# Moving the table entries of the last items of a routed attention block, and two of its ranks, to other places in GpSimd's, TensorE's and VectorE's order

## The reference

```python
gates = softmax(flat @ Wgate)                 # flat: 4096 tokens (in items of 256), 8 experts
_, top_inds = top_k(gates, 2)
mask = zeros((N, E), bool).at[arange(N)[:, None], top_inds].set(True)
pos = cumsum(mask, axis=0) * mask - 1         # the rank of a token in its expert
exp_in = zeros((E, capacity, d)).at[e_flat, p_eff].set(flat[t_flat])
exp_out = gelu(exp_in @ W1 + b1) @ W2 + b2
moe = zeros((N, d)).at[t_flat].add(exp_out[e_flat, p_g] * gate)
```

## Time and profile before

| | us |
|---|---|
| median of 3 runs | 1511.07 (1511.07 to 1511.7) |
| the profiled execution's own time | 1514.36 |
| its span, first to last instruction | 1512.6 |
| TensorE busy | 1397.3 (92%) |
| VectorE busy | 1063.2 (70%) |
| ScalarE busy | 898.2 (59%) |
| GpSimd busy | 651.4 (43%) |

### The profile page before, as it was taken

One profiled execution on the slowest core, in us unless ns is written; L12 is line 12 of the kernel. 1 busy time (PEld: TensorE's weight loads), 2 busy tenths in 40 slices (PEclk: granted clock), 3 DMA queues, 4 the chain that ended last, 5 costly groups with the idle time before them and its releaser, 6 DMA issues.

```text
span 1512.6 us, 26340 instructions
## 1 busy us (share of the span) xinstructions
PE 1397.3 (92%) x9265; PEld 1190.9 (79%) x9265; DVE 1063.2 (70%) x2514; ACT 898.2 (59%) x2092; POOL 651.4 (43%) x624
## 2 busy tenths in 40 slices
PE   7987899999999999999999998998729999999997
PEld 5765789999999998777876776776518888888886
DVE  2998577777777776778897787885436666666654
ACT  5776355555555553378887887887626455465452
POOL 0222344344343414555556665553434435445333
PEclk9998899999999999999999999999759999999999
DMA  6421256666665633343453454442432443234212
GB/s 176 140 81 37 60 155 170 171 177 178 172 186 170 171 102 124 100 142 116 133 147 100 135 142 102 123 123 71 126 85 58 93 102 95 38 98 100 40 22 29
DMA packets 133587, 173.53 MB, mean 115 GB/s; under 512 B 20725, under 2 KB 105536, under 8 KB 133456
## 3 DMA queue, kind: packets, MB, share of 16 engines
q1 hardware_dynamic: 105296, 119.89, 24.4%
q0 software_dynamic: 28160, 51.96, 17.3%
HBM read 107.28 MB, written 42.08 MB: 99 GB/s over the span
## 4 chain that ended last, share of the span: by engine, by line
PE 74%; DVE 8%; issue 6%; DMA 5%; ACT 3%; POOL 2%; another core or an unknown queue 1%; SPq 1%; POOLq 0%; DVEq 0%; ACTq 0%
PE banks L941 33%; PE banks L1983 8%; PE banks L1470 5%; PE banks L1514 4%; DMA xe<-pooled,idx 4%; PE banks L1985 4%; PE banks L1567 4%; PE banks L1003 3%; PE banks L451 2%; PE banks L1527 2%; PE banks L1488 1%; PE banks L1529 1%; PE banks L1959 1%; DVE row_at L516 1%
## 5 line engine op out<-in xcount | busy, mean ns | idle before, releaser
L941 PE MATMUL banks<-hi_x,hi_w 128*128 128x320 f32 (+1 forms) x832 | 289.4, 348 | 9.9 <-DVE hidden L976 5.3
L941 PE MATMUL banks<-lo_x,hi_w 128*128 128x320 f32 (+1 forms) x832 | 287.6, 346 | 0.0
L941 PE MATMUL banks<-hi_x,lo_w 128*128 128x320 f32 (+1 forms) x832 | 287.6, 346 | 0.0
L882 POOL DMA_INDIRECT xe<-pooled,idx x160 | 159.1, 995 | 235.1 <-DVE hidden L976 104.4
L1618 ACT ACTIVATE PN<-banks,smax 128x256 f32<-128x256 f32 (+1 forms) x512 | 180.3, 443 | 11.9 <-DVE smax L1724 11.9
L1443 POOL DMA_INDIRECT got<-done,slot x128 | 125.6, 981 | 143.3 <-DVE smax L1724 71.4
L1983 PE MATMUL banks<-down_w,hi_h 128*128 128x512 f32 x512 | 183.8, 401 | 0.0
L1944 POOL DMA_INDIRECT out<-X,tab x64 | 100.1, 1565 | 187.1 <-DVE X L2048 157.7
L941 PEld LDWEIGHTS banks<-hi_x,hi_w 128*128 128x128 f32 x832 | 159.6, 192 | 25.1 <-issue 8.0
L941 PEld LDWEIGHTS banks<-hi_x,lo_w 128*128 128x128 f32 x832 | 159.3, 192 | 13.7
L941 PEld LDWEIGHTS banks<-lo_x,hi_w 128*128 128x128 f32 x832 | 159.7, 192 | 12.3
(11 more groups left out here) (194 smaller groups left out, 3299.7 us busy)
## 6 DMA issues: line engine op xcount, KB each, us to landing
w<-in_L_ffn_w SPq DMA_DIRECT2D x96, 256.0 KB
done<-res SPq DMA_DIRECT2D x31, 640.0 KB
BIG<-in_L_ffn_W SPq DMA_DIRECT2D x16, 1024.0 KB
QS<-parts_qk SPq DMA_DIRECT2D x48, 256.0 KB
KS<-parts_qk SPq DMA_DIRECT2D x96, 128.0 KB
mask<-in_c_masks SPq DMA_DIRECT2D x16, 257.0 KB, 2.9
pooled<-XF SPq DMA_DIRECT2D x16, 256.0 KB, 3.2
WS<-in_L_cond_W SPq DMA_DIRECT2D x16, 256.0 KB
```

The source lines that it names most:

```text
L882: e.indirect_dma_start(xe[:, n % NXE, i, :], None, pooled, bass.IndirectOffsetOnAxis(ap=idx0[:, n * NS0 + i:n * NS0 + i + 1], axis=0)).the ...
L941: last = e.matmul(o, a[i], b[j], start=start and k == 0, stop=stop and k == 2, skip_group_check=True)
```

## The change

The tables change, and the step "entry" gets two more names, so that one table can hold an item's entries at two places.

- POOL_ROUND gets ("late", -3, 1 to 3) and ("ahead", -2, 0 and 1) between ("base", -2) and the gathers. The dictionary spread names those entries of items 10 to 13 that run there in place of their old places: (10, 1 to 3), (11, 1 to 3), (12, 1 to 3), (13, 0) and (13, 1). Each of them, and (13, 2) and (13, 3) in the drain, also waits for a given count of row maxima (one, (12, 2), for a count of gate logits).
- Of the eight (14, i), those with i = 1, 3, 5 and 7 wait for the outputs of item 15 turned (s_o_ps 31), scaled (s_at 32), turned back (s_at_turned 16) and for its projection (s_proj 16).
- In the drain the four (15, i) stand ahead of ("norm", 15, 1) instead of behind it.
- ("rank", 14) moves ahead of ("values", 15, 2) and ("gate", 14), ("rank", 15) ahead of ("proj", 15); ("place", 14) moves ahead of the last row maximum, ("place", 15) ahead of VectorE's ("proj", 15).

```diff
 POOL_ROUND
-        ("got", 3, 0, 3), ("got", 3, 1, 0), ("norm", -1, 1), ("got", 3, 1, 1), ("norm", 2, 0), ("entry", -3, 1),
+        ("late", -3, 1), ("late", -3, 2), ("late", -3, 3), ("ahead", -2, 0), ("ahead", -2, 1), ("got", 3, 0, 3), ("got", 3, 1, 0), ("norm", -1, 1), ("got", 3, 1, 1), ("norm", 2, 0), ("entry", -3, 1),
 POOL_LAST
-        *(("entry", 13, i) for i in range(TB * K1)), *(("entry", 14, i) for i in range(R * K1)), ("norm", 15, 1),
-        *(("entry", 15, i) for i in range(TB * K1)), *(("entry", 16, i) for i in range(TB * K1)))
+        ("entry", 13, 2), ("entry", 13, 3), *(("entry", 14, i) for i in range(R * K1)), *(("entry", 15, i) for i in range(TB * K1)),
+        ("norm", 15, 1), *(("entry", 16, i) for i in range(TB * K1)))
@@
+    ENTRY_PACE14 = {1: (s_o_ps, TB * 15 + 1), 3: (s_at, TB * 15 + 2), 5: (s_at_turned, 16), 7: (s_proj, 16)}
+    LATE = B - 6
+    entry_pace = {(b, i): (s_smax, 3 * NG * (b + 3) + n) for b in range(LATE, B - 4) for i, n in ((1, 1), (2, 4), (3, 6))}
+    entry_pace.update({
+        (12, 1): (s_smax, 3 * NG * 15), (12, 2): (s_lgs, 14), (12, 3): (s_smax, 3 * NG * 15 + 1), (13, 0): (s_smax, 3 * NG * 15 + 4),
+        (13, 1): (s_smax, 3 * NG * 15 + 7), (13, 2): (s_smax, 3 * NG * 15 + 10), (13, 3): (s_smax, 3 * NG * 15 + 12)})
+
+    spread = {a: "late" for a in entry_pace if a[0] < 13}
+    spread.update({(13, 0): "ahead", (13, 1): "ahead"})
@@
-            elif step == "entry" and entry_at(b, d[0]):
+            elif step in ("entry", "late", "ahead") and step == spread.get((b, d[0]), "entry") and entry_at(b, d[0]):
...
+                if (b, d[0]) in entry_pace:
+                    e.wait_ge(*entry_pace[b, d[0]])
+                if b == 14 and d[0] in ENTRY_PACE14:
+                    e.wait_ge(*ENTRY_PACE14[d[0]])
```

More of the change, by code:

```diff
@@ L1211, in _build @@
         ("scores", 15, 3, 0), ("turn_p", 15, 2, 2), ("scores", 15, 3, 1), ("values", 15, 1), ("turn_p", 15, 2, 0),
-        ("turn_p", 15, 2, 1), ("gate_turn", 14), ("scores", 15, 3, 2), ("values", 15, 2), ("gate", 14),
-        ("turn_p", 15, 3, 2), ("rank", 14), ("turn_p", 15, 3, 0), ("turn_p", 15, 3, 1), ("values", 15, 3),
-        ("outputs", 15, 0), ("outputs", 15, 1), ("out_turn", 15), ("proj", 15), ("rank", 15), ("gate_turn", 15),
-        ("gate", 15), ("rank", 16))
+        ("turn_p", 15, 2, 1), ("gate_turn", 14), ("scores", 15, 3, 2), ("rank", 14), ("values", 15, 2), ("gate", 14),
+        ("turn_p", 15, 3, 2), ("turn_p", 15, 3, 0), ("turn_p", 15, 3, 1), ("values", 15, 3),
+        ("outputs", 15, 0), ("outputs", 15, 1), ("out_turn", 15), ("rank", 15), ("proj", 15),
+        ("gate_turn", 15), ("gate", 15), ("rank", 16))
     DVE_LAST = (
         ("route", 13, 3), ("row_max", 15, 2, 0), ("proj", 14), ("row_max", 15, 2, 1), ("norm", 14, 1),
-        ("row_max", 15, 2, 2), ("scale", 14, 1), ("row_max", 15, 3, 0), ("row_max", 15, 3, 1), ("row_max", 15, 3, 2),
-        ("base", 14), ("gate", 14), ("route_shift", 14), ("place", 14), ("route", 14, 1), ("outputs", 15, 0), ("outputs", 15, 1),
-        ("route", 14, 2), ("route", 14, 3), ("proj", 15), ("norm", 15, 1), ("base", 15), ("scale", 15, 1), ("place", 15), ("gate", 15),
-        ("route_shift", 15), ("route", 15, 1), ("route", 15, 2), ("route", 15, 3), ("place", 16))
+        ("row_max", 15, 2, 2), ("scale", 14, 1), ("row_max", 15, 3, 0), ("row_max", 15, 3, 1), ("place", 14),
+        ("row_max", 15, 3, 2), ("base", 14), ("gate", 14), ("route_shift", 14),
+        ("route", 14, 1), ("outputs", 15, 0), ("outputs", 15, 1), ("route", 14, 2), ("route", 14, 3), ("place", 15),
+        ("proj", 15), ("norm", 15, 1), ("base", 15), ("scale", 15, 1), ("gate", 15), ("route_shift", 15), ("route", 15, 1),
+        ("route", 15, 2), ("route", 15, 3), ("place", 16))
     ACT_LAST = (
```

## The result

The changed kernel takes 1502.98 us as the median of 10 runs (1501.45 to 1508.52) and the kernel before 1511.46 beside it (10 runs, 1507.16 to 1515.7). The ratio is 0.995, 95% interval 0.9936 to 0.9964, so 5.4 to 9.7 us are gained, where 3.4 were forecast. The profiled execution took 1504.43 us, 9.9 less than the one of before.

The account below looks back on a forecast made before the run. TensorE was taken to bound the full rounds, a chain of waits the drain. T at -8.0 us (-1.0, -3.5, -3.5) and the norm at +4.6 gave -3.4: 1507.7 us as median, chance 0.45, range 1503.5 to 1514.0.

Parts of the forecast that it names:

- the stall at 1023.49 gone: Round 13: moving (10, 1 to 3) from behind the norms removes oT's 1.10 us wait; 1.0 us gained.
- round 15: Rounds 14 and 15: breaking up the run of four entries from 1046.62 gains 3.5 us, bounds 0 and 5.9.
- drain up to T: Drain before item 15's outputs: fewer entries there shorten waits of a row maximum and a weights copy; 3.5 us gained.
- T: Moment VectorE can start on item 15's outputs, 1090.14 before; forecast 8.0 us sooner, between 1080 and 1084.
- place 14 ahead of the last row maximum: Drain, VectorE: seven small instructions of 1.13 us, hidden by ScalarE's exponentials; cost 0, at most 1.2 us.
- norm of item 15: Drain, GpSimd: eleven entries ahead of it make it start at T + 14.0, not T + 9.4; 4.6 us lost.
- a bound of 6.0 us: Most the drain up to T could gain: 17.40 us less TensorE's 11.82, plus some 0.4 for a better clock.
- that case: Behind T: if the chain ran faster at a better clock, 14.0 us of entries would keep the norm in place.
- the fourth case: Rival: all stalls from round 13 to T go, T gains 11.5 us, sum -6.9, 1504.2 us; chance 0.13.
- Lone entries stall too: Rival: each entry at the sensitive place costs 1.75 us, two stalls stay in round 15 and drain; 1511.2 us, chance 0.25.
- the forecast's sign for it: Sign of a wrong gain: oT's wait of 1.7 us back in round 15 beside (12, 0).
- The late norm alone: Rival: entries aren't the cause, stalls stay, T gains at most 1 us; +3.6 to +4.6, about 1515.2 us; chance 0.17.

Follow-up runs that it names:

- n1: Changed kernel with the norm of item 15 ahead of the four (15, i), still behind all eight (14, i): 1495.2 us, ratio 0.9906 to the kernel before.
- n2: Changed kernel with the norm of item 15 ahead of (14, 5): 1494.05 us, ratio 0.9898 to the kernel before; timed again on another chip, 1499.17 us, 0.9914.
- t_ranks_only: Kernel before with only the ranks and places of the drain moved as in the change, GpSimd untouched: 1516.45 us, ratio 1.0057.
- m_none: Kernel before without entries 1 to 3 of items 2 to 9 (24 of 64): 1477.9 us against 1478.96.
- m_early: Kernel before with all four entries of each full round ahead of base, between gathers: 1478.36 us, ratio 0.9992; on another chip 1515.79 us, 1.0013.

## Why the prediction was right, and where it was short

The sign was right, and the time lies in the range, but the gain is about twice the forecast. Step by step:

| step | forecast | measured |
|---|---|---|
| the stall at 1023.49 gone | -1.0 | -1.18, and -0.28 in the piece before |
| round 15 | -3.5 | -3.95 (-5.7 in n1 and n2_again, at full clock) |
| drain up to T | -3.5 | -6.25 |
| place 14 ahead of the last row maximum | 0 | nothing that shows (+3.1 where entries stay in rows, t_ranks_only) |
| norm of item 15 | T + 14.0, +4.6 | T + 14.76, +5.34 |
| sum | -3.4 | -6.3 by the pieces; -5.4 to -9.7 by the ratio |

**The step that failed is the drain's term.** The forecast took 3.5 of a bound of 6.0 us, for two waits that it saw (3.0 and 1.78 us) less an overlap, and gave the clock 0.4 us. But the same 95 or 96 matmuls take TensorE 10.10 us at a granted clock of 0.77 (kernel before, chip D) and 8.25 us at 1.00 (after). So up to 1.85 us of the drain was clock, and in the first trace more (10.86 us at 0.77). The clock fell at 1079.93 (1082.50 in the first trace), behind the waits of the row maximum, and with the waits gone it stays up to T. Both went together: 6.25 us, which even passes the bound of 6.0, since that gave the clock 0.4 alone. The full clock also shortened what is behind T: XR starts 4.96 us behind it, before 7.37. The forecast had named that case and said rightly that it would not help the norm, since the eleven entries are the longer path: 1075.24 + 11 x 1.274 = 1089.25, and the norm starts at 1089.26. Its T + 14.0 missed only the 0.74 us from T to the first of them, which waits for the same turning of outputs as T itself does.

**The rivals.** By its number the fourth case, all stalls gone, came about: T gains 11.5 us there, 11.66 here, and 1504.2 us against 1502.98. It had 0.13. That it fits so well is in part luck, as its terms were 1.1, 5.9 and 4.5 us and the pieces give 1.46, 3.95 and 6.25. The argument against it, that the last group's chain has no other work beside it, is true but was no bound: the same chain takes 10.2 us on every chip when no row of entries runs beside it. *Lone entries stall too* fell in round 14, which holds four spaced entries and takes 25.32 us, 25.33 on a chip without stalls, and in the drain; in round 15 the forecast's sign for it, a wait on oT, came back with 1.00 us, but only where the clock was low. *The late norm alone* has its price paid on chip C, +4.3 us by the ratio, where it said +3.6 to +4.6. Its cause was another, though: it left the stalls in their places, and chip C has none. So on each sort of chip another of the forecast's rivals has the better number, and the forecast between them is true on neither.

The Trainium skill, "SBUF — State Buffer", section "SBUF: two separate sides", leaves an entry no way to hold ScalarE back inside that memory. On chips B and C the traces agree. On A and D, and in the first traces, ScalarE's oT starts late beside entries (1.77 us in the earlier trace rows), and the lateness moves when the entries move; whether that goes through the memory or through a semaphore, of which the section doesn't speak, the traces don't tell.

**What the prediction's signs said.** No remote wait above 1 us from round 13's end to T, GpSimd not idle before the norm, eleven entries ahead of it, the last four waiting for slots: all there. One was missed: T was to be between 1080 and 1084, and is 1078.5 even without the 3.98 us of the execution itself.

## What to carry to other kernels

When waits and a low clock stand together in a stretch, and one cause is taken away, price both as gone, as in this drain; the halfway value of a bound needs a reason of its own. On an engine that works in order, a run of short things put ahead of one thing on the critical path costs their number times their pitch: before placing them, ask which of them the end really waits for (here the last four of the table waited for their slots anyway; moving the norm ahead of seven gave some 7.8 us more on chip A, and n2's ratios of 0.9898 and 0.9914 on chips A and D stand against the changed kernel's 0.995, which wasn't run on those two). And a gain of half a per cent that comes from taking away a disturbance should be measured on more than one chip, since the disturbance may not be there.

## What the runs showed of the hardware

One program, the kernel before, takes 1508.58 and 1512.49 us on two chips and 1478.96 and 1478.34 on two others, 2.2% apart, where the 17 and 15 executions on chips B and C lie within 0.4%. The pieces say where. From item 1's mark to T the kernel before takes 404.22 us on chip D (683.32 to 1087.54) and m_none 374.17 on chip B (681.21 to 1055.38); from the end of the last table entry to the end of the span it is 396.1 and 396.0 us. (m_none leaves 24 entries out; the changed kernel on chip C, with all of them, takes 374.55 us to T.) So nearly all of the difference lies in the stretch where entries are written. The granted clock is not its cause: in the kernel before it is 1.00 in full rounds on chip D as in those of m_early on chip B, and in the drain on chip D it falls at 1079.93, behind a wait of 3.26 us that ended at 1075.70. Most entries of 128 pairs of 8 bytes cost GpSimd 0.97 us and 0.30 us to the next, 1.27 us, on every chip; the rest take 1.0 to 1.2 us and a few 1.50.
